# Last columns of several scans copied to the carried states by one instruction

## What is computed

```python
dA = jnp.exp(delta[..., None] * A)                       # A: 1024 channels x 16 states
dBu = (delta * u)[..., None] * Bm[:, :, None, :]

def step(h, t):
    dA_t, dBu_t, C_t = t
    h = dA_t * h + dBu_t
    return (h, jnp.einsum('bdn,bn->bd', h, C_t))
_, ys = lax.scan(step, h0, (dA, dBu, Cm))                # over 4096 positions, from h0 = 0
y = jnp.swapaxes(ys, 0, 1) + u * Dp
y = y * jax.nn.silu(z)
return y @ wout.T
```

## Time and profile before

| | us |
|---|---|
| median of 3 runs | 7713.24 |
| profiled execution | 7717.63 |
| its span | 7715.8 |
| scan stage, from first to last scan | 232.6 to 7288.7 |
| PE busy | 6892.4 (89%) |
| DVE busy | 7095.9 (92%) |
| ACT busy | 6131.3 (79%) |
| POOL busy | 6975.0 (90%) |

### The profile page before, as it was taken

The page is one execution under the profiler, slowest core; times in us unless marked ns, Lnnn a source line. Parts: engine busy times, 40 slices in busy tenths (PEclk is TensorE's granted clock), DMA queues, the critical chain, the costliest instruction groups (busy, mean ns, idle before and its releaser), DMA issues. The chain is left out here.

```text
span 7715.8 us, 140260 instructions
## 1 busy us (share of the span) xinstructions
PE 6892.4 (89%) x32680; PEld 4031.5 (52%) x32680; DVE 7095.9 (92%) x11547; ACT 6131.3 (79%) x11641; POOL 6975.0 (90%) x3806
## 2 busy tenths in 40 slices
PE   6899888999898889999898899998888999998889
PEld 3455555555555555555555555555555555555445
DVE  1799999999999999999999999999999999999766
ACT  1788888888788888888788888888888888888645
POOL 0899999999999999999899999999999999999768
PEclk8999999999999999999999999999999999999989
DMA  5444445444444453444445535444455344444555
GB/s 165 141 133 131 128 140 146 118 126 137 127 132 126 145 146 100 145 132 132 124 130 147 147 98 147 130 134 132 123 147 147 102 143 130 132 132 126 146 198 171
DMA packets 597312, 1049.15 MB, mean 136 GB/s; under 512 B 113456, under 2 KB 221872, under 8 KB 588016
## 3 DMA queue, kind: packets, MB, share of 16 engines
q1 hardware_dynamic: 594384, 1038.78, 45.7%
q10 hardware_dynamic: 2080, 1.05, 0.0%
HBM read 909.69 MB, written 129.91 MB: 135 GB/s over the span
## 5 line engine op out<-in xcount | busy, mean ns | idle before, releaser
L623 POOL TENSOR_TENSOR dBu<-Bb,du 128x1024 f32<-128x1024 f32 x2048 | 4797.4, 2365 | 15.6 <-DVE h L1138 11.7
L753 ACT ACTIVATE dA<-delta,A 128x512 f32<-128x512 f32 x4096 | 2777.0, 693 | 540.3 <-DVE hR L1138 228.2
L1138 DVE TENSOR_TENSOR_SCAN h<-dA,state,dBu 128x512 f32<-128x512 f32 x1792 | 2310.1, 1289 | 314.1 <-ACT dA L753 259.7
L974 PE MATMUL yT<-ident,hC 128*128 128x128 f32 x9216 | 1437.5, 284 | 412.5 <-DVE hC L1154 395.7
L632 POOL TENSOR_TENSOR hR<-hR,Cb 128x512 f32<-128x512 f32 x1024 | 1303.5, 1273 | 354.1 <-DVE state L1168 354.1
L974 PEld LDWEIGHTS yT<-ident,hC 128*128 128x128 f32 x9216 | 1067.5, 144 | 784.7 <-DVE hC L1154 621.6
L1138 DVE TENSOR_TENSOR_SCAN hR<-dA,state,dBu 128x512 f32<-128x512 f32 x1024 | 1292.3, 1262 | 7.1 <-ACT dA L753 7.1
L1154 DVE TENSOR_TENSOR hC<-h,Cb 128x512 f32<-128x512 f32 x1792 | 1216.1, 679 | 0.0
L967 PE MATMUL bg<-u,comb 128*128 128x512 f32 x2112 | 989.1, 594 | 0.9 <-DVE u L1096 0.9
L928 PE MATMUL bg<-hT,win_z 128*128 128x512 f32 x2048 | 966.5, 594 | 15.4 <-ACT sp_a L649 15.4
L1138 DVE TENSOR_TENSOR_SCAN hV<-dA,state,dBu 128x512 f32<-128x512 f32 x768 | 966.9, 1259 | 5.6 <-ACT dA L753 3.3
(11 more groups left out here) (159 smaller groups left out, 8479.1 us busy)
## 6 DMA issues: line engine op xcount, KB each, us to landing
comb<-pre_scratch SPq DMA_DIRECT2D x1040, 256.0 KB, 4.6
Bb<-bc_scratch SPq DMA_DIRECT2D x264, 512.0 KB, 8.4
Cb<-bc_scratch SPq DMA_DIRECT2D x264, 512.0 KB, 7.6
win_u<-in_win SPq DMA_DIRECT2D x264, 256.0 KB, 4.3
pre_scratch<-pre SPq DMA_DIRECT2D x264, 256.0 KB, 3.4
comb<-comb_scratch SPq DMA_DIRECT2D x66, 1024.0 KB, 7.0
win_z<-in_win SPq DMA_DIRECT2D x257, 256.0 KB, 2.7
part_scratch<-pre SPq DMA_DIRECT2D x132, 256.0 KB, 2.0
```

The lines of the kernel that those rows point to most:

```text
L623: pool.tensor_tensor(dBu[:, q % AHEAD], Bb[:, 2 * q:2 * q + 2, :], du[:, j % 2, :].unsqueeze(1).broadcast_to([P, 2, T]), ALU.mult).then_in ...
L753: act.activation(dA[dA_bank(v, j, n)][:], delta[:, j % 2, :], ACT.Exp, scale=A[:, v % 2, j * N + n:j * N + n + 1]).then_inc(dA_made, 1)
L974: ins = nc.tensor.matmul(yT[:, tt * P:(tt + 1) * P], product[:, tt * P:(tt + 1) * P], ident[:], start=first and tt == 0, stop=False, is_tr ...
L1138: nc.vector.tensor_tensor_scan(to, dA[dA_bank(v, j, n)][:], dBu[:, q % AHEAD, k, :], state[:, c:c + 1], ALU.mult, ALU.add).then_inc(h_made, 1)
```

## The change

1. Scans 3 and 4 lie in neighbouring places of hR, and one instruction at the end of step 2 copies both last columns. Scans 7 and 11 are copied as before. The product of GpSimd for scan 3 and its adding by TensorE move from step 4 to step 5, since JOINS now goes by the step of the copy.
2. hV gets three places, one per turned scan, and one instruction at the end of step 4 copies the columns of 1, 5 and 9 to states four columns apart.
3. The bank h and the three dA banks become one PSUM tensor `scans`, in which h stands before dA0. Where the in-place scan of a last pair (12,13 or 14,15) is in dA0, one instruction copies two columns, each from its own bank; in the other two of three cases the two copies stay.
4. `side_saved` is split in two: `aside_saved`, which rises three times a pass, and `turned_saved`, once.

```diff
-JOINS = {n: min(n // 2 + LATE, NQ - 1) for n in ASIDE}
-HC, HR, HV = 4, 4, 2
+
+COPIES = ((3, 4), (7,), (11,))
+KEPT_WITH = {n: ns[-1] for ns in COPIES for n in ns}
+JOINS = {n: min(KEPT_WITH[n] // 2 + LATE, NQ - 1) for n in ASIDE}
+HC, HR, HV = 4, 4, 3
...
-        dA = [ps(f"dA{k}", [P, T]) for k in range(3)]
-        h = ps("h", [P, T])
+
+        scans = ps("scans", [P, 4, T])
+        h, dA = scans[:, 0, :], [scans[:, k + 1, :] for k in range(3)]
...
-                                    k = (j * NA + ASIDE.index(n)) % HR
-                                    pool.wait_ge(side_saved, side(g, n) + 1 + A0)
+                                    k = ASIDE.index(n)
+                                    pool.wait_ge(aside_saved, copied(g, n) + A0)
...
-                                    dve.wait_ge(bg_ready, ready(i if t >= 0 or j else i - 1, f"T{before}"))
-
-                                    dve.wait_ge(side_saved, g * (NA + NT) + (len([k for k in SIDE if k <= TURNED[t]]) + A0 if t >= 0 else
-                                                len([k for k in SIDE if k <= TURNED[t + NT]]) + A0 - (NA + NT)))
+                                    dve.wait_ge(bg_ready, ready(i if j else i - 1, f"T{((j - 1) % MT) * N + n}"))
+
+                                    dve.wait_ge(turned_saved, g + V0)
...
-                                    nc.vector.tensor_copy(state[:, c:c + 1], h[:, T - 1:T])
-                                    nc.vector.tensor_copy(state[:, c + 1:c + 2],
-                                                          dA[dA_bank(v, j, n + 1)][:, T - 1:T]).then_inc(state_saved, 1)
+                                    if dA_bank(v, j, n + 1) == 0:
+                                        nc.vector.tensor_copy(state[:, c:c + 2], scans[:, 0:2, T - 1]).then_inc(state_saved, 1)
+                                    else:
+                                        nc.vector.tensor_copy(state[:, c:c + 1], h[:, T - 1:T])
+                                        nc.vector.tensor_copy(state[:, c + 1:c + 2],
+                                                              dA[dA_bank(v, j, n + 1)][:, T - 1:T]).then_inc(state_saved, 1)
...
+                                for ns, places, saved in [(ns, hR, aside_saved) for ns in COPIES] + [(TURNED, hV, turned_saved)]:
+                                    if n != ns[-1]:
+                                        continue
                                     dve.wait_ge(h_made, g * N + n + 1 + H0)
...
+                                    k = (ASIDE if places is hR else TURNED).index(ns[0])
+                                    step = ns[1] - ns[0] if len(ns) > 1 else 1
+                                    nc.vector.tensor_copy(state[:, j * N + ns[0]:j * N + n + 1:step],
+                                                          places[:, k:k + len(ns), T - 1]).then_inc(saved, 1)
```

More of the change, by code:

```diff
@@ L57 @@
 NG = P // GROUP
-assert MT * NS % HC == 0 and MT * NA % HR == 0 and MT * NT % HV == 0
+assert MT * NS % HC == 0 and HR == NA and HV == NT
+assert all(b - a == ns[1] - ns[0] for ns in (*COPIES, TURNED) for a, b in zip(ns, ns[1:]))
+assert sorted(n for ns in COPIES for n in ns) == sorted(ASIDE)
 GENERAL = [
@@ L340, in scan_stage @@
         dA_made, dBu_made, h_made = sem("dA_made"), sem("dBu_made"), sem("h_made")
-        hR_made, hR_used, side_saved = sem("hR_made"), sem("hR_used"), sem("side_saved")
+        hR_made, hR_used, aside_saved, turned_saved = (sem("hR_made"), sem("hR_used"), sem("aside_saved"),
+                                                       sem("turned_saved"))
         hC_made, hC_used, state_saved, state_kept = (sem("hC_made"), sem("hC_used"), sem("state_saved"),
@@ L346, in scan_stage @@
         block = ctx.enter_context(nc.Block())
-        H0, C0, U0, R0, S0, A0, K0, Z0, O0, DU0 = 2 * AHEAD, HC, HC, HR, 1, HR + HV, MT, 1, 16, 1
+        H0, C0, U0, R0, S0, A0, V0, K0, Z0, O0, DU0 = 2 * AHEAD, HC, HC, HR, 1, len(COPIES), 1, MT, 1, 16, 1
         ready = lambda i, name: i * EV + (PRO + NUM[name] + 1)
@@ L356, in scan_stage @@
         aside = lambda g, n: g * NA + len([k for k in ASIDE if k < n])
-        side = lambda g, n: g * (NA + NT) + len([k for k in SIDE if k < n])
+        copied = lambda g, n: g * len(COPIES) + len([ns for ns in COPIES if ns[-1] <= KEPT_WITH[n]])
         KEEPING = [q for q in range(NQ) if 2 * q in STRAIGHT or 2 * q + 1 in STRAIGHT]
@@ L826, in _ @@
                                 act.wait_ge(state_saved, kept(g, 0) + S0)
-                                act.wait_ge(side_saved, g * (NA + NT) + A0)
+                                act.wait_ge(aside_saved, g * len(COPIES) + A0)
+                                act.wait_ge(turned_saved, g + V0)
                                 act.mul(state[:, last * N:(last + 1) * N], state[:, last * N:(last + 1) * N],
@@ L1064, in _ @@
                                     pe.wait_ge(hR_made, aside(g, n + 1))
-                                    add_state(hR[:, (j * NA + ASIDE.index(n)) % HR, :], False).then_inc(hR_used, 1)
+                                    add_state(hR[:, ASIDE.index(n), :], False).then_inc(hR_used, 1)
                             for n in (2 * q, 2 * q + 1):
@@ L1123, in _ @@
                                     dve.wait_ge(hR_used, aside(g, n) + 1)
-                                    to = hR[:, (j * NA + ASIDE.index(n)) % HR, :]
+                                    to = hR[:, ASIDE.index(n), :]
                                 elif n in TURNED:
-                                    t = TURNED.index(n) - HV
-                                    before = j * N + TURNED[t] if t >= 0 else ((j - 1) % MT) * N + TURNED[t + NT]
-                                    dve.wait_ge(bg_ready, ready(i if t >= 0 or j else i - 1, f"T{before}"))
-                                    dve.wait_ge(side_saved, g * (NA + NT) + (len([k for k in SIDE if k <= TURNED[t]]) + A0 if t >= 0 else
-                                                len([k for k in SIDE if k <= TURNED[t + NT]]) + A0 - (NA + NT)))
-                                    to = hV[:, (j * NT + TURNED.index(n)) % HV, :]
+                                    dve.wait_ge(bg_ready, ready(i if j else i - 1, f"T{((j - 1) % MT) * N + n}"))
+                                    dve.wait_ge(turned_saved, g + V0)
+                                    to = hV[:, TURNED.index(n), :]
                                 elif n in IN_PLACE:
```

12 lines of the change are left out of this document (2 added, 10 removed).

## The result

| | median us | runs, us | against the kernel before |
|---|---|---|---|
| before | 7713.42 | 7, 7710.40 to 7719.01 | |
| changed | 7738.91 | 7, 7732.96 to 7741.79 | 1.0031 [1.0021, 1.0042] |

The account below looks back on a forecast made before the run. No single engine bounds the kernel; the chain changes engines within a chunk. Gains by pass sum to 1.81 us a chunk, times 32 chunks is 58 us, giving 7656 us, range 7608 to 7700.

Parts of the forecast that it names:

- kind 1: Copy of turned scan 1 at step 0, hidden under hC's tail: removing it worth 0, bounds 0 to 0.12 us.
- kinds 2 and 3: Removed copies of scan 3 at step 1, worth 0.06 us, and scan 5 at step 2, worth 0.34 us.
- The line on what would prove me wrong: Wrong if 0.28 us stays, two-bank or three-column copies visibly exceed 0.15 us, or VectorE waits for dBu.
- "No loss" for GpSimd: GpSimd makes hR(3) behind dBu(5); its own work of 26.0 us a pass still fits.
- The copy over two PSUM banks at the price of one copy: Last pairs: two copies become one, 172 in all, worth 0.06 us each; not visibly longer than 0.15 us.
- Scan 5's 0.34 us: Step 2: without scan 5's copy, scan 6 starts 1.23 us behind scan 5, not 1.57.
- In pass 4, forecast 0.35: VectorE is the chain in pass 4, TensorE has a few tenths of slack: gain 0.35 us a chunk.
- Pass 2 0.43 and pass 3 0.40 by the later join: Moving hR(3)'s join to step 5 shortens TensorE's chain: 0.43 us in pass 2, 0.40 in pass 3.
- passes 0 and 1 together, forecast 0.2 shorter: TensorE works without a gap into pass 1, so VectorE's savings mostly lengthen waits: 0.2 us taken for both.
- pass 5 -0.25 where 0.07: Pass 5: dA(8) is already 0.07 us late from TensorE's U projection, the rest is eaten; gain taken 0.07 us.
- pass 7 0.07 where 0.30: Pass 7: VectorE is the chain in most chunks, ScalarE in a quarter; gain taken 0.30 us.
- The slower rival, SyncE's reload queue: Pass 7 reloads of B and C wait for hR(3), 2.4 us later: +19 us, 7732 us; chance 0.04.

Follow-up runs that it names:

- the sixth kernel: Kernel before with turned columns copied by reduction and last pairs over two PSUM banks; scans 3 and 4 apart, old joins: 7684.18 us, 0.9960.
- the seventh: The sixth kernel with hR(3) made and joined one step later in passes 2 and 3 alone: 7675.13 us, 0.9946.
- second: Changed kernel with its two several-column copies from SBUF written as a maximum reduction over an axis of length one (the kernel by reduction): 7683.22 us, 0.9960.
- first experiment: Changed kernel with its copies from SBUF made column by column, 5 one-column copies for 2 joint ones: 7678.90 us, 0.9955.
- the third experiment: Kernel before with only the three turned columns joined in one copy at step 4; scans 3 and 4 copied apart, old joins: 7814.68 us, 1.0132.

## Why the prediction was wrong

The step that failed is the last sentence of kind 1: "The same holds for the copy of turned scans at step 4, which stays and grows to three columns; two more columns cost nothing that is on the path", with its bounds of 0 to 0.12 us. It took the row of a one-column copy for the price of a three-column one. What it measured is 0.156 to 1.31 us by what GpSimd runs, 100 us for it and its two-column sister together over what a reduction takes, 56 to 60 us of them on the path. The same holds for the two-column copy of kinds 2 and 3. The bounds came from the place (behind hC's tail) and didn't ask what else the instruction needs. The line on what would prove me wrong named it, but no rival had a price for it. "No loss" for GpSimd was true of its own work (idle before hR 354.1 us in the earlier trace rows, 353.5 after) and beside the point: it is GpSimd's running instruction that holds VectorE.

Point by point:

- 10607 instructions of VectorE in place of 11547: right. Scan 2 still 0.72 us behind hC(0), scan 6 1.23 us behind scan 5 (1.57 in the earlier trace rows): right. VectorE of the changed kernel, pass 5:

```profile
3024.30 0.68 DVE L1159 TENSOR_TENSOR hC<-scans,Cb 128x512 f32<-128x512 f32 x1
3025.02 1.29 DVE L1143 TENSOR_TENSOR_SCAN scans<-scans,state,dBu 128x512 f32<-128x512 f32 x1
...
3029.83 1.25 DVE L1143 TENSOR_TENSOR_SCAN hV<-scans,state,dBu 128x512 f32<-128x512 f32 x1
3031.00 0.14 DVE L1177 COPY state<-hR 128x2 f32<-128x2 f32 x1
3031.06 1.28 DVE L1143 TENSOR_TENSOR_SCAN scans<-scans,state,dBu 128x512 f32<-128x512 f32 x1
```

- The copy over two PSUM banks at the price of one copy: right, 145 ns.
- Scan 5's 0.34 us on the path in pass 7: right, 26.37 to 26.01 where the joins stay; in the changed kernel too in the chunks with the clock up, 26.36 to 26.05 on their medians. In pass 4, forecast 0.35: wrong, 26.46 to 26.41. There scan 9 waits for ScalarE's dA, as at 3008.85 in the rows above (0.36 us). Before, it waits in 9 of 32 chunks; in the changed kernel and in that by reduction in every one, 0.34 and 0.36 us on the mean, as much as VectorE won. The mean of pass 4 does fall by 0.37 (26.79 to 26.42 by reduction), but it falls by 0.33 with the pairs alone, where scan 5's copy stays: these are mainly the six long passes above, not scan 5. Had it been read as the forecast come true, that would have been luck.
- Pass 2 0.43 and pass 3 0.40 by the later join: right in size and place (27.18 to 26.74, 27.14 to 26.70). But passes 0 and 1 together, forecast 0.2 shorter, are 0.19 longer (53.56 to 53.75 in the kernel by reduction). The join is not the cause: the sixth kernel, with the old joins, has 53.78, and the seventh 53.90. It moves the border between the two passes by some 0.4 and leaves their sum. On the means the two passes take 53.76 before and 53.81 by reduction: where TensorE has no gap, VectorE's savings gave nothing at all, and the 0.2 was a term without a row behind it.
- So of 58 us the change without its blocked copies keeps 30 to 34 (second and first experiment). The account is 58 us forecast, less 24 to 28 for mis-sized passes, less 56 to 60 for the blocked copies, and a loss of 26; it closes because both parts are differences of measured times. What is in the first part, by the means of the kernel by reduction: passes 0 and 1 give -0.05 us where 0.20 was taken, pass 5 -0.25 where 0.07, pass 7 0.07 where 0.30, which is 0.8 us a chunk or 26 us; the other passes together give 0.14 more than was taken. In pass 7 it is the clock, 7 more long chunks than before; in pass 5 the wait before scan 8 grew from 0.28 to 0.62 us on the mean. Of TensorE's clock the prediction says nothing.
- The slower rival, SyncE's reload queue, had the direction and the wrong mechanism: GpSimd's dBu waits 3.2 us in all for the reloaded B (1.8 before), and VectorE's scans 4.0 us for dBu in the changed kernel (first lines of the two fences of groups above).

## What to carry to other kernels

- On VectorE, count the columns and the memories of a copy before joining small copies: from SBUF to SBUF those of two and of three float32 columns waited for whatever GpSimd was running, those of one column in no case seen here. Where GpSimd is busy most of the time, copy column by column, or from PSUM, or move the columns with a reduction over an axis of length one.
- Such a wait has no price of its own; it is the rest of the other engine's instruction at the moment of the start. It changes with every reordering of that engine, so read it from both timelines, not from a mean.
- A join moved for all passes pays in those where its engine bounds the next pass, and elsewhere it can cost: the later dBu held the first scan of pass 2, and pass 7 was long twice as often. Move it where the table of pass lengths says so.
- If a pass has two lengths, look at the granted clock of its first microseconds before explaining the difference by waits; a median over chunks then jumps with the share of long ones.

## What the runs showed of the hardware

- Copy of 3 columns, SBUF to SBUF, float32: 156 to 160 ns with GpSimd idle or about to end, and the rest of GpSimd's instruction plus 22 to 33 ns otherwise, up to 1.31 us; 2 columns: 141 ns on the median, or up to 528.
- The same columns by a reduction over an axis of length one: 149 and 130 ns on the mean beside the same GpSimd work. The Trainium skill, "SBUF — State Buffer", section "Who interferes with whom", says that such a reduction never contends on this chip; the trace agrees.
- In the changed kernel 138 of the 140 three-column copies that began in the last 47 to 85 ns of GpSimd's hR were done in 160 ns or less; the other two waited for the whole of the next instruction, 1.3 us.
- GpSimd's instructions do not get longer by it: delta takes 1275 ns on the mean in the changed kernel, 1276 before; dBu 2365 in both.
- TensorE's granted clock changes between its two levels within passes, and a pass 7 or 4 that starts at the lower one is longer than one that doesn't: pass 7 by 0.8 to 1.9 us in all traces but that of the third experiment, pass 4 by 1.4 to 1.7 us in that of the kernel before.
